# One row scatter under way at a time on POOL in a fused two-layer kernel with routed experts

## The chip, the cores and the metric

The kernel runs on 1 core of one Trainium2 chip. The metric is the device time in microseconds (us) of one execution; the number quoted for a kernel is the median of its runs.

## The reference

Two transformer-like layers over `x` of shape (4, 1024, 128) in f32, each with an adaptive layernorm ahead of its two halves. In both layers the second half is a mixture of experts with top-2 routing over 8 experts:

```
# layer 0: causal attention with 16 heads, then
scores = softmax(x @ gate_w.T); w = scores * top2_mask(scores)
out = sum_e w[:, e] * down_e(silu(gate_e(x)) * up_e(x)) + sigmoid(x @ sgate) * shared(x)
# layer 1: a state-space block (S4D kernel, FFT convolution, GLU), then
scores = x @ Wg.T; w = scores of the top 2
out = sum_e w[:, e] * W3_e(silu(W1_e x) * (W2_e x))
```

There are 4096 tokens, so 8192 rows (token, choice) go to experts in each layer. The change concerns only how these rows reach the experts.

## The kernel before, in words

The kernel computes only the two experts that a token chose. It does so by sorting rows in memory. Each of the 4 batches (1024 tokens, `TPB` = 8 tiles of 128 tokens) is normalised into `w.h[0]` (rows of 130 words: 128 values, an id and a weight), copied to `w.h[1]` by ACT (`second_copy`, which counts `h_kept`), scored on PE, and DVE works out for each row its place in the row store `d.xg[layer]` (`places`, which counts `slots_done`). Then POOL issues `scatter(pool, n)` for n = 0 to 63: one indirect DMA each, that takes 128 rows of 520 bytes from SBUF and writes each to its place in DRAM. Sixteen of them belong to a batch and count on one semaphore `scattered[b]`, 16 for each. The first of a batch waits for `h_kept` and `slots_done`; the other fifteen wait for nothing.

The experts (`experts_parts`) then run over `NSLOT` = 72 slots of 128 rows, in order. SP loads slot n into `xt` (line 1725), eight slots ahead at most (it waits for `y_done`, n - 7). It may start on the slots of a wave only when all batches of that wave are scattered: `WAVES` is [(2, 40), (3, 72)] for layer 0 (slots 0 to 39 need batches 0 to 2) and [(1, 24), (2, 40), (3, 72)] for layer 1 (slots 0 to 23 need batches 0 and 1). PE transposes the slot (`t_in`, L1844), makes gate and up products (L1852 in layer 0, L1858 in layer 1), ACT the silu, DVE the product (`product(n)`, L1795 and following, which first copies the ids of the rows to `place[:, n % 8]`), PE the down product (L1869), ACT scales into `yo[n % 8]` (`y_copy(n)`, L1767), and POOL scatters `yo` to `d.yk` (`experts.scatter`, L1738). `place` and `yo` have 8 buffers, so `product(n)` and `y_copy(n)` wait until y scatter n - 8 has landed:

```
after(dve, y_out[n % UN], 16 * (n // UN))   # product(n)
after(act, y_out[n % UN], 16 * (n // UN))   # y_copy(n)
```

PE, DVE and ACT take the steps of all slots in a fixed order, with one or two slots between the stages; in layer 0 the first 12 slots also carry the rest of the shared expert (`late_tensor` and its like), work that stands in the same fixed order.

The order on POOL sets what is queued behind a scatter. In layer 0 all 64 row scatters come first and the 72 y scatters after them. In layer 1 `ROWS_AHEAD` = 40 row scatters come first, then y scatter n and row scatter 40 + n take turns:

```
ahead = 2 * NT if layer == 0 else ROWS_AHEAD
for n in range(ahead):
    routed.scatter(pool, n)
for n in range(NSLOT):
    experts.scatter(pool, n)
    if ahead + n < 2 * NT:
        routed.scatter(pool, ahead + n)
```

Of the kernel before, what the change touches and what calls it, by code (L numbers as in the profile page):

```python
# [18 lines left out]
TPB = T // P  # L19
# [1088 lines left out]
def route_parts(nc, w, d, layer, ctx, bank, gate):  # L1108
# [57 lines left out]
    scattered = w.scattered[layer]  # L1166
# [71 lines left out]
    def scatter(pool, n):  # L1238

        t, k = divmod(n, 2)  # L1240
        b = t // TPB
        if n % (2 * TPB) == 0:
            pool.wait_ge(h_kept, b + 1)
            pool.wait_ge(slots_done, b + 1)
        nc.gpsimd.indirect_dma_start(out=d.xg[layer], out_offset=bass.IndirectOffsetOnAxis(ap=w.slot[:, k, t:t + 1], axis=0),  # L1245
                                     in_=w.h[k][:, t, :], in_offset=None).then_inc(scattered[b], 16)

# [411 lines left out]
    made.hid_done = hid_done  # L1659
    made.sync, made.gpsimd, made.vector, made.scalar, made.tensor = sync_part, gpsimd_part, vector_part, scalar_part, tensor_part  # L1660
    made.scatter, made.tables, made.tail, made.tails_out = scatter, tables, tail, tails_out
    made.tables_set, made.ranked, made.w_read, made.w_copied, made.sh_out = tables_set, ranked, w_read, w_copied, sh_out
    return made
# [1153 lines left out]
```

## Time and profile before

| what | us |
|---|---|
| median of 3 runs (1256.02 to 1265.23) | 1263.59 |
| the profiled execution, its own time | 1261.72 |
| its span, first to last instruction | 1260.2 |
| PE busy | 962.0 (76%) |
| DVE busy | 830.9 (66%) |
| ACT busy | 695.9 (55%) |
| POOL busy | 444.4 (35%) |

The rows are times of one profiled execution in us from the start of its span. 1.5 us of its time lie outside the span. An engine's share is an average over attention (to about 540 us), layer 0's routing and experts (to about 833), the state-space block (to about 935), layer 1's routing (to about 1047), its experts (to about 1233) and the last sums.

### The profile page before, as it was taken

The page shows a single profiled execution, that of the slowest core. Times are in us where ns is not written, and L with a number is a line of the kernel's source. Part 1 is how long each engine was busy: PE and PEld are TensorE (multiplying, and loading weights), DVE is VectorE, ACT ScalarE, POOL GpSimd, SP SyncE. Part 2 cuts the span into 40 slices and gives each one's busy share as a digit, 9 for nine tenths or more (in the row PEclk, how much of TensorE's full clock was granted, in tenths as well). Part 3 has the DMA queues.
Part 4 walks back from the last instruction along what each step waited for, and adds up shares of the span by engine and source line. Part 5 has one row for each costly group of instructions (what it writes and reads, how often), then busy time and mean ns, then how long its engine had stood idle before and what let it go on. Part 6 is the DMA issues. An engine that isn't in the chain of part 4 may idle for free. (4 is left out here: it accounts for less than half of the span.)

```text
span 1260.2 us, 26930 instructions
## 1 busy us (share of the span) xinstructions
PE 962.0 (76%) x9019; PEld 631.0 (50%) x9019; DVE 830.9 (66%) x2082; ACT 695.9 (55%) x1479; POOL 444.4 (35%) x510
## 2 busy tenths in 40 slices
PE   4565899999999999957748977827578446779990
PEld 2232343333434333445436766727455336779990
DVE  6797998999999999376523445447867444323445
ACT  3684477877877777734324555528024333446660
POOL 5617122323212221216652356520001462664441
PEclk9795699999999999966779989868778657999995
DMA  7236011111111100021111122257552321222226
GB/s 208 67 110 226 7 61 53 51 35 49 53 38 36 46 8 2 2 72 61 45 53 33 43 78 77 69 195 228 137 149 64 87 71 31 63 76 69 66 57 208
DMA packets 101694, 97.16 MB, mean 77 GB/s; under 512 B 15181, under 2 KB 85928, under 8 KB 101560
## 3 DMA queue, kind: packets, MB, share of 16 engines
q1 hardware_dynamic: 87320, 75.29, 20.2%
q0 software_dynamic: 8704, 17.97, 4.2%
q10 hardware_dynamic: 5536, 2.18, 0.6%
q8 instruction: 76, 1.25, 0.4%
q14 instruction: 58, 0.48, 0.1%
HBM read 60.18 MB, written 34.95 MB: 75 GB/s over the span
## 5 line engine op out<-in xcount | busy, mean ns | idle before, releaser
L569 DVE TENSOR_REDUCE part<-sps 128x2 f32<-128x1024 f32 (+2 forms) x307 | 327.5, 1114 | 27.1 <-PE sps L557 15.3
L912 ACT ACTIVATE prob<-tpa 128x1024 f32<-128x1024 f32 (+1 forms) x208 | 192.8, 927 | 45.2 <-PE tpa L858 43.3
L1738 POOL DMA_INDIRECT yk<-yo,place x144 | 146.7, 1019 | 179.4 <-ACT yo L1767 162.0
L744 POOL TENSOR_SCALAR_AFFINE_SELECT prob<-prob 128x512 f32<-128x512 f32 x128 | 80.5, 641 | 307.2 <-ACT prob L912 307.2
L1245 POOL DMA_INDIRECT xg<-h,slot x128 | 127.7, 998 | 130.6 <-DVE slot L1396 88.9
L878 PE MATMUL ops<-prob,vs 128*32 128x512 f32 (+3 forms) x1536 | 157.9, 498 | 0.1
L912 ACT ACTIVATE prob<-tpb 128x512 f32<-128x512 f32 (+1 forms) x224 | 126.8, 566 | 36.5 <-PE tpb L858 36.4
L1795 DVE COPY place<-xt 128x1 uint32<-128x1 uint32 x144 | 22.1, 153 | 187.9 <-ACT esg L1761 97.4
L550 PE MATMUL sps<-qk 48*128 48x512 bf16 (+2 forms) x734 | 132.4, 338 | 12.6 <-DVE part L569 7.8
L1858 PE MATMUL banks<-xT,y 128*128 128x128 f32 x864 | 112.9, 282 | 21.2 <-ACT y L1752 13.9
L1858 PEld LDWEIGHTS banks<-xT,y 128*128 128x128 f32 x864 | 105.7, 197 | 24.9 <-ACT xT L1747 17.8
L858 PE MATMUL tpa<-qk 50*128 50x512 bf16 (+3 forms) x512 | 85.4, 324 | 5.2 <-ACT prob L912 5.1
L858 PE MATMUL tpb<-qk 50*128 50x512 bf16 (+3 forms) x256 | 82.5, 342 | 4.8 <-DMA qk<-mrow 3.5
L550 PEld LDWEIGHTS sps<-qk 48*128 48x128 bf16 x734 | 41.1, 94 | 73.4 <-DVE part L569 49.6
L1767 ACT ACTIVATE yo<-banks,xt 128x128 f32<-128x128 f32 x144 | 53.0, 368 | 42.8 <-PE banks L1869 34.1
L1852 PE MATMUL banks<-xT,up_at 128*128 128x128 f32 (+1 forms) x432 | 67.2, 296 | 5.1 <-DVE up_at L1789 3.0
L557 PE MATMUL sps<-half 64*128 64x128 bf16 x976 | 66.5, 207 | 0.0
L858 PEld LDWEIGHTS tpa<-qk 50*128 50x128 bf16 x512 | 28.0, 94 | 69.4 <-ACT prob L912 61.2
L1844 PE MATMUL banks<-ident,xt 128*128 128x128 f32 x144 | 41.8, 292 | 27.3 <-ACT xT L1747 12.6
L1852 PEld LDWEIGHTS banks<-xT,up_at 128*128 128x128 f32 (+1 forms) x432 | 58.4, 204 | 7.4 <-ACT xT L1747 4.5
L557 PEld LDWEIGHTS sps<-half 64*128 64x128 bf16 x976 | 51.6, 97 | 20.8 <-issue 2.0
L1761 ACT ACTIVATE esg<-banks 128x384 f32<-128x384 f32 x72 | 35.5, 493 | 47.4 <-PE banks L1858 41.5
(356 smaller groups left out, 1878.7 us busy)
## 6 DMA issues: line engine op xcount, KB each, us to landing
xt<-xg SPq DMA_DIRECT2D x144, 65.0 KB
qk<-term SPq DMA_DIRECT2D x24, 256.0 KB, 2.7
qk<-qk SPq DMA_DIRECT2D x64, 96.0 KB
arena<-kpad SPq DMA_DIRECT2D x6, 1024.0 KB, 11.0
powers<-powr SPq DMA_DIRECT2D x8, 516.0 KB, 5.3
powr<-powers SPq DMA_DIRECT2D x4, 1032.0 KB, 9.0
qk<-qk SPq DMA_DIRECT2D x64, 64.0 KB
h<-yk SPq DMA_DIRECT2D x8, 512.0 KB, 7.3
```

Of the source, the lines that this page charges most:

```text
L550: ins = nc.tensor.matmul(out[:, s, at * wd:(at + 1) * wd], qk[lo:lo + KR, 0, x, i * P:(i + 1) * P], qk[lo:lo + KR, 1, x, c0:c0 + wd], star ...
L557: ins = nc.tensor.matmul(out[:, s, (at + 1) * wd - P + 64 * u:(at + 1) * wd], w.half[lo:lo + 64, 0, u, :], w.half[lo:lo + 64, 1, u, 64 * u ...
L569: return nc.vector.tensor_reduce(to, src, AX.X, ALU.max, negate=True)
L744: nc.gpsimd.affine_select(out=blk, in_=blk, pattern=[[0, HQ], [1, P]], compare_op=ALU.is_ge, fill=0.0, base=0, channel_multiplier=-1).then ...
L858: ins = nc.tensor.matmul(slot_of(t, m)[:, bank, col:col + n], qk[t % 4][lo:lo + KR + 2, 1, x, j * P:(j + 1) * P], qk[t % 4][lo:lo + KR + 2 ...
L878: ins = nc.tensor.matmul(ops[32 * h:32 * h + 32, o0:o0 + n], vs[t % 2][:, j, h, :], prob[:, PBUF[c] * HQ + u, col:col + n], start=c in OPE ...
L912: nc.scalar.activation(prob[:, at:at + len(units), 0:n], slot_of(t, m)[:, :, 0:n], ACT.Exp, scale=float(HD) ** -0.5).then_inc(exp_done, 1)
L1245: nc.gpsimd.indirect_dma_start(out=d.xg[layer], out_offset=bass.IndirectOffsetOnAxis(ap=w.slot[:, k, t:t + 1], axis=0), in_=w.h[k][:, t, : ...
L1738: nc.gpsimd.indirect_dma_start(out=d.yk, out_offset=bass.IndirectOffsetOnAxis(ap=place[:, u:u + 1], axis=0), in_=yo[u][:], in_offset=None) ...
L1767: nc.scalar.activation(yo[n % UN][:], pd[n % 2], ACT.Copy, scale=xt[n % UN][:, C + 1:C + 2]).then_inc(y_done, 1)
L1852: ins = nc.tensor.matmul(pg[n % 2][0:cw, m * P:(m + 1) * P], up_at[n % WST][:, m * P:m * P + cw], xT[n % 4][:], start=True, stop=True)
L1858: ins = nc.tensor.matmul(out[:, m * P:(m + 1) * P], up_at[n % WST][:, (k * M + m) * P:(k * M + m + 1) * P], xT[n % 4][:], start=True, stop ...
```

## The change

Each row scatter but the very first of a layer waits, before it is issued, until the row scatter ahead of it has landed, that is until `scattered` of its batch has got the 16 counts of each scatter up to it. The y scatters get no wait, and no other wait is changed.

```diff
@@ -1242,6 +1242,8 @@
         if n % (2 * TPB) == 0:
             pool.wait_ge(h_kept, b + 1)
             pool.wait_ge(slots_done, b + 1)
+        if n > 0:
+            pool.wait_ge(scattered[(n - 1) // (2 * TPB)], 16 * ((n - 1) % (2 * TPB) + 1))
         nc.gpsimd.indirect_dma_start(out=d.xg[layer], out_offset=bass.IndirectOffsetOnAxis(ap=w.slot[:, k, t:t + 1], axis=0),
                                      in_=w.h[k][:, t, :], in_offset=None).then_inc(scattered[b], 16)
```

## Rows read from the trace of the kernel before

**Rows 1.** The page's groups of instructions, the two kinds of scatter on POOL.

```profile
L1738 POOL DMA_INDIRECT yk<-yo,place x144 | 146.7, 1019 | 179.4 <-ACT yo L1767 162.0
L1245 POOL DMA_INDIRECT xg<-h,slot x128 | 127.7, 998 | 130.6 <-DVE slot L1396 88.9
```

**Rows 2.** Timeline of POOL, layer 0: start, duration, what, [idle before <- releaser].

```profile
564.81 1.20 POOL L1245 DMA_INDIRECT xg<-h,slot  x1 [18.92 <-DVE slot L1396]
...
567.79 1.46 POOL L1245 DMA_INDIRECT xg<-h,slot  x1 [0.30 <-issue]
569.55 0.96 POOL L1245 DMA_INDIRECT xg<-h,slot  x1 [0.30 <-issue]
...
635.10 0.96 POOL L1245 DMA_INDIRECT xg<-h,slot  x1 [0.30 <-issue]
...
665.69 0.96 POOL L1245 DMA_INDIRECT xg<-h,slot  x1 [0.30 <-issue]
```

**Rows 3.** The chain that ended last, 1225 to 1240: start, duration, piece.

```profile
1232.57 2.23 DMA yk<-yo,place
...
1234.88 3.93 DMA h<-yk
```

**Rows 4.** Timeline of all engines around two wakings of POOL.

```profile
645.76 0.17 DVE L1396 CAST slot<-slf 128x16 uint32<-128x16 f32 x1
...
646.72 0.96 POOL L1245 DMA_INDIRECT xg<-h,slot  x1 [10.66 <-DVE slot L1396]
...
672.82 0.37 ACT L1767 ACTIVATE yo<-banks,xt 128x128 f32<-128x128 f32 x1 [0.34 <-PE banks L1869]
...
673.46 0.96 POOL L1738 DMA_INDIRECT yk<-yo,place  x1 [6.81 <-ACT yo L1767]
```

**Rows 5.** Timeline of SP: first loads of slots, layer 0 and layer 1.

```profile
638.83 8.54 SPq L1725 DMA_DIRECT2D xt<-xg  x8
...
1026.74 2.60 SPq L1725 DMA_DIRECT2D xt<-xg  x3
```

**Rows 6.** Timelines of PE, ACT and DVE, layer 0's first slots.

```profile
655.57 0.27 PE L1844 MATMUL banks<-ident,xt 128*128 128x128 f32 x1
664.52 1.62 PE L1852 MATMUL banks<-xT,up_at 128*128 128x128 f32 x6
...
675.54 0.27 ACT L1747 COPY xT<-banks 128x128 f32<-128x128 f32 x1 [0.40 <-PE banks L1844]
...
696.38 0.15 DVE L1795 COPY place<-xt 128x1 uint32<-128x1 uint32 x1 [1.11 <-ACT esg L1759]
```

**Rows 7.** Timeline of POOL, layer 1's row scatters and its first y scatter.

```profile
971.15 0.99 POOL L1245 DMA_INDIRECT xg<-h,slot  x1 [35.81 <-DVE slot L1396]
...
1023.19 0.96 POOL L1245 DMA_INDIRECT xg<-h,slot  x1 [0.30 <-issue]
...
1057.49 0.96 POOL L1738 DMA_INDIRECT yk<-yo,place  x1 [16.47 <-ACT yo L1767]
1058.75 0.96 POOL L1245 DMA_INDIRECT xg<-h,slot  x1 [0.30 <-issue]
```

**Rows 8.** Timelines of PE and DVE, layer 1's first slots.

```profile
1050.13 2.90 PE L1858 MATMUL banks<-xT,y 128*128 128x128 f32 x12 [2.30 <-DVE y L1789]
...
1074.34 0.13 DVE L1795 COPY place<-xt 128x1 uint32<-128x1 uint32 x1
```

**Rows 9.** DMA issues by line: KB each, median us to landing.

```profile
flip<-in_flip SPq DMA_DIRECT2D x1, 64.0 KB, 1.9
```

**Rows 10.** Timelines of ACT, PE and DVE: long idle times during trains of row scatters.

```profile
636.01 0.60 ACT L1464 ACTIVATE sg<-banks 128x512 f32<-128x512 f32 x1 [13.06 <-remote]
...
993.31 1.09 PE L1570 MATMUL banks<-ident,h 128*128 128x128 f32 x4 [13.23 <-issue]
...
1022.50 0.22 DVE L1349 COPY lg<-banks 128x64 f32<-128x64 f32 x1 [10.09 <-DMA kpad<-gate]
```

**Rows 11.** Two stretches of layer 1: length, busy PE, PEld, DVE, ACT, POOL, PEclk.

```profile
1057.00:1137.00 80.00, 61.45 (x491) 58.19 (x490) 27.23 (x98) 32.91 (x100) 48.58 (x49) 0.96 0.24 69
1137.00:1229.00 92.00, 91.44 (x820) 91.23 (x819) 37.65 (x128) 61.12 (x174) 42.50 (x44) 1.00 0.22 62
```

## The prediction

> **What bounds the kernel now.** I read the costliest groups first, for how much of POOL the scatters are: 128 row scatters of 998 ns mean and 144 y scatters [rows 1]. By the mean alone POOL is idle two thirds of the time, so the question is not its load but who waits for the last scatter of a train. For that I read POOL's timeline. Inside a train the row scatters follow one another with 0.96 us of work and 0.30 us between, 1.26 us apart; a few of the first take up to 1.46 us [rows 2]. A batch of 16 is gone in about 20 us. The next batch's places are ready later than that in every case, so POOL waits for DVE at each batch head (88.9 us in all, [rows 1]). The scatters are now hidden behind the routing.
>
> Then come the two readers of a train's end. SP's first load of a slot in layer 0 is issued at 638.83 [rows 5], 3.73 us after the last scatter of batch 2 was issued at 635.10 [rows 2]. PE transposes that slot only at 655.57, and the first products with it start at 664.52 [rows 6]: the routing of batch 3 and the shared expert fill the time, so there are some 15 us of slack before the transpose and 24 before the products. In layer 1 SP starts at 1026.74 [rows 5], 3.55 us after batch 1's last scatter (1023.19, [rows 7]), and the products start at 1050.13 [rows 8]: slack of some 20 us. The second reader is the y scatter behind all row scatters on POOL's queue. Layer 0's first y scatter starts at 673.46 [rows 4], after the last row scatter of 665.69 [rows 2]; layer 1's at 1057.49 [rows 7]. And `product(8)` waits for that first y scatter to land, at 696.38 in layer 0 [rows 6] and 1074.34 in layer 1 [rows 8]: slack of some 20 and 15 us.
>
> **The pitch under the change.** One row scatter may start only when the one ahead has landed. No row shows the landing of a row scatter, so I bound it. The last y scatter, of the same form and nearly the same size, starts at 1232.57 and its DMA piece lasts 2.23 us; SP issues what waited for it at 1234.88 [rows 3]. The 3.73 and 3.55 us above contain the landing and SP's own steps ahead of a load (it has a register to read), so they are upper bounds. POOL's waking adds to it. A y scatter that waits for one semaphore starts 0.27 us after ACT's copy ends (672.82 + 0.37 to 673.46, [rows 4]). A row scatter at a batch head, with several waits ahead of it, starts 0.79 us after the places (645.76 + 0.17 to 646.72, [rows 4]). The new wait stands alone ahead of 15 of 16 scatters, so I take the y scatter's 0.27. The pitch p is then 2.23 + 0.27 = 2.50 us in place of 1.26. Low end: 2.3, the 2.23 with hardly any waking. High end: 2.8, from waking at 0.6 or landings made later by the weight loads and by DVE (the 1.46 us scatter is such a one). A batch takes 40 us, twice what it took. The heads of layer 0's batches lay 27 us apart (564.81 to 646.72 for three, [rows 2, 4]), so from batch 1 on POOL no longer waits for DVE there: the whole train is 64 scatters in a row from 564.81.
>
> The Trainium skill has a fit for this, in "DMA: Bandwidth & Descriptors", section "Anatomy of one DMA — SWDGE (gpsimd) path": about 2.0 us fixed, mostly the receipt of the write, plus the bytes over 436 GB/s. For 66,560 bytes that would be 2.15 us, an estimate by that page, and the trace's 2.23 agrees within 0.1. By it the pitch would be 2.42 and the sum below some 7 us smaller.
>
> **Layer 0.** Two routes lead to the slots. *By SP:* the last scatter of batch 2 is the 48th and starts at 564.81 + 47 x 2.50 = 682.3. SP's load follows 3.73 later (686.0), lands 1.9 later, the time of another 64 KB load [rows 9] (687.9), and PE's transpose, ACT's copy of 0.27 each [rows 6] and their start-ups take 0.7: the products start at 688.6, where they started at 664.52. That is 24 us late. *By POOL's queue:* the 64th scatter starts at 564.81 + 63 x 2.50 = 722.3. The first y scatter is behind it, with no wait of its own left by then: it starts 1.27 later and lands 2.23 after that, at 725.8. `product(8)` waits for it; at 24 us late it would come at 720.5. So it is held 5 us more, and 29.4 against before. While DVE is held, PE can still do the transpose, the gate and up products and one down product that stand ahead in its order, and catches up 1.5 us of that. I take +28 us. The y scatters piled up then go at 1.27 apart against a slot pitch of 3.83 at that point and stop nobody. Batch 3 has landed long before slot 40 is asked for. Nothing later in layer 0 depends on row scatters, and no slack was on the way to layer 1, so all 28 us are carried on. As a function of the pitch this is the larger of 63p - 129.6 and 47p - 93.4: 15 at 2.3, 47 at 2.8.
>
> **Layer 1.** Times here are still those of before, without the shift. Batch 1's last scatter is the 32nd: 971.15 + 31 x 2.50 = 1048.7. SP's load 3.55 later (1052.2), landing 1.9 (1054.1), transpose, copies and the start of the products 1.3, since ACT also lays the up weights: 1055.4 against 1050.13 [rows 8], +5 us (31p - 72.2 in general: 0 at 2.3, where the slack is just used up, +15 at 2.8). The first y scatter comes after 40 row scatters at 971.15 + 39 x 2.50 + 1.27 = 1069.9, 12 us later than before, and lands at 1072.2; `product(8)` comes at 1074.34 + 5 = 1079.6 and does not wait. The remaining 24 row scatters take turns with y scatters: 1.26 us apart the pair takes 2.53 us (1057.49, 1058.75, [rows 7]), and the landing of the row scatter ahead is 2.23 + 0.27 = 2.50 after its start. The new wait is over as POOL gets to it. It is no cost at p = 2.50 and 24 x 0.3 = 7 us on POOL alone at 2.8, where the slots' pitch of 3.1 us leaves that much free. The pitch of 3.1 is 80 us over 491 matmuls / 19 a slot [rows 11]. Waves 1 and 2 need row scatters that are issued behind y scatters 7 and 23, ten slots before SP asks. No cost.
>
> **The sum.** 28 + 5 = 33 us on the profiled execution's 1261.72, 1295; against the median of 1263.59, which is 1.9 above it, 1297. I say 1296. With p = 2.3 it is 15 + 0, 1278; with p = 2.8 it is 47 + 15 = 62, 1324.
>
> **The rivals.** *A. POOL wakes slowly.* If the new wait costs what the batch head's does (0.79, [rows 4]) or the landing is seen only 3 us after the start, p is about 3.1. Then layer 0 loses 63 x 3.1 - 129.6 = 66 and layer 1 31 x 3.1 - 72.2 = 24: 1353. For it: row scatters have shown only this slow waking. Against: that one has more than one wait, and the y scatter with a single wait shows 0.27.
>
> *B. The long stalls go, and pay for it.* During the trains engines stand still for 10 to 13 us though the work that they wait for is done: ACT 13.06 until 636.01, PE 13.23 until 993.31, DVE 10.09 until 1022.50 [rows 10], and each ends near a train's end. If scatters in close succession hold up the other engines' signals or instructions, half the rate may free them. But the front of both layers is then bound by POOL's train, as above, so what is freed there is slack again. It could pay only among the slots: in layer 1 they take 3.1 us each while row scatters are mixed in, and 92 us over 820 matmuls / 19 = 2.13 us afterwards [rows 11]. If the whole difference on 24 slots is due to row scatters under way together with others, 24 x 1.0 = 24 us come back: 33 - 24 = 9, a time of about 1273. Against: the y scatters still overlap the row scatters there, and the rate is the same.
>
> *C. Faster than before.* A single scatter under way lands sooner than one in traffic, and the stalls of B go too. With POOL's train as the bound, the loss in layer 0 is gone at p = 2.0 (47 x 2.0 - 93.4 = 0.6), and layer 1 gains only as far as 31p - 72.2 is below zero. The sum is zero at p = 2.12, and at p = 1.9 it is -4 - 13 = -17, 1246. That needs a landing 1.6 us after the start, against 2.23 for a lone y scatter with nothing else on the queues [rows 3]. Hardly possible.
>
> *D. The wait is no wait.* If scatters land before POOL is done with them, nothing changes: 1264. The same row speaks against it.
>
> **How the numbers follow.** Forecast 0.79, A 0.10, B 0.05, C 0.02, D 0.04. A measurement of this kernel tells about 1% (12.6 us) from no change. Slower by over 1%: forecast and A, 0.89. Within 1%: B and D, 0.09. Faster: C, 0.02. The range is the forecast's bounds, 1278 to 1324, widened a little to 1274 below, toward B, and to 1328 above, toward A, which leaves out 0.2.
>
> **What the changed profile should show.** Row scatters 2.5 us apart, POOL's idle before each about 1.5 instead of 0.30, released by a DMA. Layer 0's train from 565 to about 723 without a gap for DVE, SP's first slot load near 686, the first gate and up products near 689, `product(8)` near 726 waiting for a DMA. Layer 0's last y scatter 28 us later than 831. In layer 1, relative to its first row scatter, the first products 5 us later. The stretch of mixed scatters unchanged at 3.1 us a slot. The attention stage unchanged. The prediction is wrong if the pitch is not near 2.5, if the slots after the trains run at another pitch than before, or if the 16 counts of a landing come later in traffic than for the lone scatter of the chain.

## The result and the profile after

The changed kernel takes 1327.48 us, median of 4 runs (1325.28 to 1328.07). The kernel before, run beside it, takes 1261.66. The ratio is 1.052, with a 95% interval of 1.049 to 1.056. The change makes the kernel 5% slower. The profiled execution has a span of 1325.6 us against 1260.2, 65.4 us more.

POOL first. The page's groups of the two scatters, of the changed kernel; the rows of before are [rows 1]. The line numbers are 2 higher than before, since the change adds two lines.

```profile
L1247 POOL DMA_INDIRECT xg<-h,slot x128 | 125.5, 981 | 245.5 <-DMA xg<-h,slot 181.4
L1740 POOL DMA_INDIRECT yk<-yo,place x144 | 146.3, 1016 | 133.3 <-ACT yo L1769 111.4
```

The scatters themselves cost what they did. What stood in front of a row scatter was DVE's slots, for 88.9 us; now it is the landing of the scatter ahead, for 181.4 us. The timeline of POOL in layer 0, to be held against [rows 2]:

```profile
562.93 1.20 POOL L1247 DMA_INDIRECT xg<-h,slot  x1 [18.93 <-DVE slot L1398]
...
568.31 0.96 POOL L1247 DMA_INDIRECT xg<-h,slot  x1 [1.57 <-DMA xg<-h,slot]
572.54 0.96 POOL L1247 DMA_INDIRECT xg<-h,slot  x1 [3.27 <-DMA xg<-h,slot]
...
732.77 0.96 POOL L1247 DMA_INDIRECT xg<-h,slot  x1 [1.75 <-DMA xg<-h,slot]
734.03 0.96 POOL L1740 DMA_INDIRECT yk<-yo,place  x1 [0.30 <-issue]
```

Half of the 63 steps in layer 0 are 2.57 us or shorter, but 12 are over 2.7: the scatter at 568.31 is followed only 4.23 us later. From the first to the 64th it is 169.84 us over 63 steps, a mean of 2.70. In layer 1 the first 32 take 88.36 us over 31 steps, 2.85. The chain that ended last runs through layer 1's train. It shows, for each scatter, the time from its start to its landing (the DMA pieces) and POOL's waking after it ("issue").

```profile
1010.09 2.31 DMA xg<-h,slot
1012.39 0.27 issue
...
1017.74 5.78 DMA xg<-h,slot
...
1028.86 4.57 DMA xg<-h,slot
...
1055.02 3.37 DMA xg<-h,slot
...
1072.30 2.29 DMA xg<-h,slot
...
1098.45 2.31 DMA xg<-h,slot
...
1101.78 1.82 DMA xt<-xg
```

A landing in quiet, with nothing else on the DMA queues, is 2.27 to 2.31 us after the start; POOL's waking is 0.27. Three landings of layer 1 took 5.78, 4.57 and 3.37. The DMA queues of two stretches, with packets, MB and share of the 16 DMA engines, show what stands beside the first. From 1017 to 1024 SP has issued weight loads of 176 KB each (the first three rows; the loads are on q1); from 1072.3 to 1084 there is nothing but five scatters (the last row).

```profile
q1 hardware_dynamic: 1701, 1.04, 66.6%
q0 software_dynamic: 37, 0.07, 3.7%
q8 instruction: 1, 0.02, 0.9%
...
q0 software_dynamic: 128, 0.27, 7.2%
```

The readers of the train, layer 0, timelines of SP, PE and DVE (the last row is `product(8)`); before they stood at 638.83, 655.57, 664.52 and 696.38 [rows 5, 6].

```profile
691.88 0.37 SPq L1727 DMA_DIRECT2D xt<-xg  x1
...
693.83 0.45 PE L1846 MATMUL banks<-ident,xt 128*128 128x128 f32 x1 [65.01 <-DMA xt<-xg]
...
695.25 1.13 PE L1854 MATMUL banks<-xT,up_at 128*128 128x128 f32 x4
...
736.39 0.15 DVE L1797 COPY place<-xt 128x1 uint32<-128x1 uint32 x1 [11.84 <-DMA yk<-yo,place]
```

PE stands idle for 65 us for the first slot's rows. Then the engines work on eight slots, until DVE's `product(8)` waits 11.84 us for the first y scatter to land, which was queued behind all 64 row scatters.

Layer 1, timelines of PE, ACT and DVE around the first slots, and its two stretches of slots (columns as in [rows 11]). Before, the products began at 1050.13 [rows 8].

```profile
1105.87 1.41 PE L1860 MATMUL banks<-xT,y 128*128 128x128 f32 x5 [0.37 <-ACT y L1754]
...
1130.37 0.49 ACT L1763 ACTIVATE esg<-banks 128x384 f32<-128x384 f32 x1 [4.43 <-remote]
...
1143.30 0.49 ACT L1763 ACTIVATE esg<-banks 128x384 f32<-128x384 f32 x1 [8.60 <-remote]
...
1143.83 0.15 DVE L1797 COPY place<-xt 128x1 uint32<-128x1 uint32 x1 [10.51 <-ACT esg L1763]
...
1122.00:1202.00 80.00, 55.28 (x406) 51.86 (x405) 21.94 (x77) 28.33 (x85) 49.72 (x51) 0.86 0.23 67
1202.00:1295.00 93.00, 93.00 (x826) 93.00 (x826) 37.85 (x130) 60.71 (x172) 41.24 (x43) 0.99 0.21 60
```

In 80 us in which row and y scatters take turns PE now does 406 matmuls; before it did 491 [rows 11]. The stretch behind is the same: 93 us for 826. So the 65 us split by layer as follows. From layer 0's first row scatter to its last y scatter it was 266.43 us before and is 306.90 now, +40.5. In layer 1 it was 261.42 (971.15 [rows 7] to 1232.57 [rows 3]) and is 288.03 (1010.09 to 1298.12), +26.6. Layer 0's train itself began 1.9 us sooner.

One thing did get better. The times at which DVE has a batch's slots ready, in layer 1, in the changed kernel:

```profile
1009.07 0.17 DVE L1398 CAST slot<-slf 128x16 uint32<-128x16 f32 x1
...
1056.43 0.17 DVE L1398 CAST slot<-slf 128x16 uint32<-128x16 f32 x1
```

The first and the fourth are shown; they are 47.4 us apart, where the profile of before has 76.5 (970.13 to 1046.67). Another profile of the kernel before, taken with the experiments, gives 74.4 for the same:

```profile
963.26 0.18 DVE L1396 CAST slot<-slf 128x16 uint32<-128x16 f32 x1
...
1037.66 0.17 DVE L1396 CAST slot<-slf 128x16 uint32<-128x16 f32 x1
```

The routing of layer 1 is 27 to 29 us shorter (in layer 0 57.6 us in place of 82.1), and the slots do not start sooner for it, since SP's first load waits for POOL's train.

### The profile page after: what moved, and what is told of

It is laid out like the page before. It is cut to its first block and busy times, and to the rows that moved or that the text cites. A ratio compares the mean times of both kernels' runs of the same rounds, so it can differ in the third digit from the quotient of the medians.

```text
span 1325.6 us, 26930 instructions
## 1 busy us (share of the span) xinstructions
PE 957.3 (72%) x9019; PEld 624.8 (47%) x9019; DVE 829.0 (63%) x2082; ACT 696.5 (53%) x1479; POOL 440.3 (33%) x510
## 3 DMA queue, kind: packets, MB, share of 16 engines
q10 hardware_dynamic: 5536, 2.18, 0.6%
## 5 line engine op out<-in xcount | busy, mean ns | idle before, releaser
L1247 POOL DMA_INDIRECT xg<-h,slot x128 | 125.5, 981 | 245.5 <-DMA xg<-h,slot 181.4
L1860 PE MATMUL banks<-xT,y 128*128 128x128 f32 x864 | 115.7, 286 | 21.5 <-ACT y L1754 13.1
L1860 PEld LDWEIGHTS banks<-xT,y 128*128 128x128 f32 x864 | 108.4, 201 | 24.9 <-ACT xT L1749 22.6
L1749 ACT COPY xT<-banks 128x128 f32<-128x128 f32 x144 | 37.6, 261 | 120.1 <-PE banks L1846 117.3
L858 PE MATMUL tpa<-qk 50*128 50x512 bf16 (+3 forms) x512 | 85.5, 324 | 5.2 <-ACT prob L912 5.1
L1846 PEld LDWEIGHTS banks<-ident,xt 128*128 128x128 f32 x144 | 21.1, 147 | 137.7 <-issue 132.7
L550 PEld LDWEIGHTS sps<-qk 48*128 48x128 bf16 x734 | 41.2, 94 | 73.7 <-DVE part L569 50.1
L1871 PE MATMUL banks<-down,y 128*128 (+1 forms) x432 | 62.7, 281 | 3.4 <-issue 3.4
```

Of the source, the lines that this page charges most:

```text
L550: ins = nc.tensor.matmul(out[:, s, at * wd:(at + 1) * wd], qk[lo:lo + KR, 0, x, i * P:(i + 1) * P], qk[lo:lo + KR, 1, x, c0:c0 + wd], star ...
L858: ins = nc.tensor.matmul(slot_of(t, m)[:, bank, col:col + n], qk[t % 4][lo:lo + KR + 2, 1, x, j * P:(j + 1) * P], qk[t % 4][lo:lo + KR + 2 ...
L1846: nc.tensor.transpose(pT[n % 2], xt[n % UN][:, 0:C], w.ident[:]).then_inc(in_ps, 1)
L1860: ins = nc.tensor.matmul(out[:, m * P:(m + 1) * P], up_at[n % WST][:, (k * M + m) * P:(k * M + m + 1) * P], xT[n % 4][:], start=True, stop ...
L1871: ins = nc.tensor.matmul(pd[n % 2], hid[n % WST][0:cw, m, :], wt[0:cw, m, :], start=m == 0, stop=m == M - 1)
```

## The experiments

The runs came in four groups, each on a chip of its own. The kernel before took 1256.93 us (19 runs) in the first, 1154.54 (7) in the second, 1256.92 (13) in the third and 1156.62 (11) in the fourth. So there are two kinds of chip here, called the first kind (1257) and the second or quick kind (1155); the pair of the result, at 1262, is of the first kind. Each ratio below is against the kernel before on the same chip; spans and single times are compared within a kind of chip only, except where the text compares the kinds. All edits are to the changed kernel, unless it says otherwise.

### The wait in one layer only (first group)

```diff
-        if n > 0:
+        if n > 0 and layer == 0:      # the second run: layer == 1
```

> Only layer 0's row scatters wait for the landing ahead. My theory (the cost of each layer is its own train's length, less the slack ahead of the slots) expects 1261.7 + 40 = about 1301: the changed kernel's layer 1 began its row scatters 38.9 us later than before. In the profile product(8) of layer 0 waits for the first y scatter's landing near 736, and layer 1 looks as before. A rival, that the two layers' costs are not independent (traffic or clock carried over), would give something clearly away from 1301.

> Only layer 1's row scatters wait. My theory expects 1261.7 + 26 = about 1288: 17 us of it before the first products (the train of 32 at a mean pitch of 2.85 us against the routing), 10 us among the first slots, where POOL works off the y scatters that piled up. Together with the layer-0-only kernel the two costs should add up to the whole 66 us, within 4.

Layer 0 alone: 1298.1 (1293.61 to 1302.12), ratio 1.031 (1.026 to 1.037), 41.2 us. Layer 1 alone: 1282.11 (1281.12 to 1285.49), ratio 1.021 (1.015 to 1.026), 25.2 us. Together they are 66.4, which is the whole change within the spread of the runs. The layers' costs add up, and they agree with the +40.5 and +26.6 read from the trace. With layer 0's front as it was, layer 1 alone shows a like loss among its slots: from the first products to the last y scatter it takes 190.1 us (1061.80 to 1251.91), where the kernel before needs 182.4.

### Two row scatters under way, and a wait ahead of every second one (first group)

The first keeps two under way. A row scatter waits for the landing of the last but one; as the two halves k of a tile alternate, each half counts on a semaphore of its own.

```diff
-        if n > 0:
-            pool.wait_ge(scattered[(n - 1) // (2 * TPB)], 16 * ((n - 1) % (2 * TPB) + 1))
+        if n > 1:
+            pool.wait_ge(scattered[(n - 2) // (2 * TPB)][k], 16 * ((n - 2) % (2 * TPB) // 2 + 1))
```

> Each row scatter waits for the landing of the one before the last, so two may be under way (each batch's counts split over two semaphores, by the choice k). Theory: the cost is the landing latency in series; with two under way the pitch is the larger of 1.27 and 2.54 / 2 = 1.27, so no change: 1262 within 6 us, with the long idle times of the routing stages as before. Rival (the long idle times of the other engines come from an unbounded number of scatters under way): the routing stage of layer 1 shortens from 76 us to under 60, and the time falls by 10 us or more.

It took 1251.54 (1245.02 to 1261.41), ratio 0.996 (0.992 to 0.999), within the 6 us of this group's kernel before. POOL's timeline in layer 0:

```profile
575.68 0.95 POOL L1247 DMA_INDIRECT xg<-h,slot  x1 [0.58 <-DMA xg<-h,slot]
576.94 0.95 POOL L1247 DMA_INDIRECT xg<-h,slot  x1 [0.30 <-issue]
578.22 0.95 POOL L1247 DMA_INDIRECT xg<-h,slot  x1 [0.33 <-DMA xg<-h,slot]
```

A landing of 2.3 us and a waking of 0.27 make 2.57 us, just over two pitches of 1.26. So with two under way nearly every wait is over as POOL comes to it. So a wait and its semaphores cost nothing here; what costs is that only one scatter is under way. The routing is not freed either: in layer 1 the slots of the four batches still take 74.2 us (964.67 to 1038.88).

The second leaves out every other wait:

```diff
-        if n > 0:
+        if n > 0 and n % 2 == 0:
```

> Only every second row scatter waits for the landing ahead, so they come in pairs, 3.81 us a pair, a mean pitch of 1.9 us. Theory (the train's length against the routing that frees up at a lower rate of scatters): the last needed scatter of layer 0 comes at 564.8 + 23 x 3.81 + 1.27 = 653.7 and the first products at about 660 against 664.5; in layer 1 the first products come 14 us earlier than before: together 5 + 14 = 19 us faster, about 1243 (1235 to 1255). Rival (the routing stages speed up only if scatters are strictly one at a time): they stay at about 82 and 76 us and the time is that of before, 1262, within 6 us.

It took 1257.14 (1250.25 to 1262.34), ratio 1.000 (0.997 to 1.003), where 1243 was expected. The time is the rival's, but the rival's reason, a routing that stays as it was, is not what happened. The routing is freed as expected: layer 1's four batches of slots take 49.5 us (966.50 to 1016.02). But the train came out slower than the pairs at its start suggest:

```profile
967.52 0.99 POOL L1247 DMA_INDIRECT xg<-h,slot  x1 [34.37 <-DVE slot L1398]
968.81 0.97 POOL L1247 DMA_INDIRECT xg<-h,slot  x1 [0.30 <-issue]
971.40 0.96 POOL L1247 DMA_INDIRECT xg<-h,slot  x1 [1.61 <-DMA xg<-h,slot]
```

A pair is 3.88 us, so 1.94 a scatter; the first 32 took 67.6 us (967.52 to 1035.16), 2.18 each. The products begin 75.06 us after the first scatter, 3.9 sooner than before and not 14. Of the 27 us of routing that this frees, POOL's train gives 4 on; in layer 0 the products begin only 0.5 us sooner (99.24 after the first scatter against 99.71), and not 5. My expectation had taken the landings in quiet for all of them; most of its error in time is that.

### Every third, more row scatters behind the y scatters, fewer weight loads, an earlier wave (second group)

This chip runs the kernel before in 1154.54 us. No profile of the kernel before was taken on it.

```diff
-        if n > 0:
+        if n > 0 and n % 3 == 0:
```

> The new wait stands ahead of every third row scatter only, so three may be under way and the next group starts when the last of them has landed. Theory (spacing frees the routing, but the train then sets the end): the mean pitch is (2 x 1.26 + 2.5)/3 = 1.68 us, or some 1.9 with the late landings that the run with every second wait showed; no train is then later than the fronts need. If the long stalls of the routing go with the pauses, its fourth batch has its slots 25 us after the first scatter minus nothing: the last slots_done at about 622 in layer 0 and 1018 in layer 1 as with every second wait, and the first products of layer 1 come near 1038, the time 1245 to 1250. Rival (the stalls depend on how many row scatters are under way at once): with three under way the last slots come at about 645 and 1046 as in the kernel before, and the time is that of before, 1257.

1189.86 (1186.44 to 1192.71), ratio 1.031 (1.027 to 1.035). Both theories had 1245 or more, on a chip like the first. Against this chip's own time, the kernel is 3% slower though it waits ahead of only one scatter in three. Neither theory's time holds here. The slots of layer 1's four batches take 51.9 us (932.34 to 984.25), but that does not decide for the theory: on a quick chip the routing takes 49.2 us even with two scatters always allowed under way (fourth group, below).

```diff
-                ahead = 2 * NT if layer == 0 else ROWS_AHEAD
+                ahead = 48 if layer == 0 else ROWS_AHEAD
```

> The changed kernel, but in layer 0 48 of the 64 row scatters stand ahead of the first y scatter on POOL's queue in place of all 64; the other 16 take turns with the y scatters. Theory (layer 0's loss is the larger of two routes, and the one by POOL's queue is 11 us longer than that by SP's first load): product(8) is held no more until the first y scatter lands at 736, layer 0's first products stay at about 695, its last y comes 7 to 10 us sooner, and the time is about 1319 in place of 1327. Rival (turns of y and row scatters cost among the slots what layer 1 showed, some 0.4 us a slot or more): the 16 turns give the gain back, and the time stays within 3 us of 1327.

1276.54 (1275.14 to 1280.98), ratio 1.107 (1.102 to 1.111). The changed kernel without this edit wasn't run on this chip. Its nearest relative is the next one, which has the same queue in layer 0. There the first y scatter starts at 733.05 and `product(8)` at 735.41; here they stand at 701.42 and 724.65. DVE's timeline shows it, first in this kernel, then in the next:

```profile
724.65 0.15 DVE L1797 COPY place<-xt 128x1 uint32<-128x1 uint32 x1 [1.11 <-ACT esg L1761]
```

```profile
735.41 0.15 DVE L1797 COPY place<-xt 128x1 uint32<-128x1 uint32 x1 [12.03 <-DMA yk<-yo,place]
```

The wait of 12 us is gone, and `product(8)` comes when the slots' own pitch brings it. From the first row scatter to the last y scatter of layer 0 it is 273.3 us (563.20 to 836.51) against 288.9 (561.16 to 850.08). The products begin 131.0 and 132.0 us after the first row scatter, so 1.0 of the 15.6 is not the queue's. The route by POOL's queue costs some 14 us over SP's on this chip, and the 16 turns between the slots did not eat that up. The 14 is rough, since the two kernels differ in their weight loads too. Those are also why the whole times differ by only 5.3 us: with half the loads layer 1 is 8.6 us shorter (261.9 against 270.5). In the first pair of profiles it is less: the first products are 32.6 late and the end of layer 0 40.5, so 7.9, where 16p - 36.2, the difference of the prediction's two lines, gives 7.0 at 2.70. Both routes exist, and the one by POOL's queue is the longer.

```diff
             if e >= WB:
-                sp.wait_ge(w_tr, place(e - WB) + 1)
+                return
```

The last run of this kind leaves out the weight loads of experts 4 to 7 (and counts `w_in` without them).

> The changed kernel without the weight loads of experts 4 to 7 in both layers; their slots use the weights of experts 0 to 3, so the output is another one. All scatters, waits and products stay. Theory (the landings that take 3.4 to 5.8 us instead of 2.3 are late because of weight loads that SP issues during a train): the pitch falls to 2.55 throughout, the 32nd scatter of layer 1 starts 79 us after its first instead of 88, the 64th of layer 0 161 us after its first instead of 170, and the time is about 1327 - 9 - 9 = 1309. Rival (they are late because of instruction fetches or of something else): the late landings stay, the mean pitch stays at 2.70 and 2.85, and the time at 1322 to 1328.

1281.87 (1279.36 to 1284.47), ratio 1.110 (1.106 to 1.114). In layer 1 the first 32 row scatters take 83.25 us (990.03 to 1073.28), 2.69 each; with all the loads, in the kernel just above, 87.33 (975.50 to 1062.83), 2.82 each. POOL's longest idle time inside layer 1's train fell from 3.96 to 3.03, first with all the loads, then with half:

```profile
988.45 0.96 POOL L1247 DMA_INDIRECT xg<-h,slot  x1 [3.96 <-DMA xg<-h,slot]
```

```profile
1009.94 0.96 POOL L1247 DMA_INDIRECT xg<-h,slot  x1 [3.03 <-DMA xg<-h,slot]
```

These are single profiles, and the same 32 scatters take 88.36, 85.51 and 86.23 in the other three profiles with all the loads and every wait in layer 1. So weight loads are 2 to 5 us of the lateness in layer 1, where I had put 9. In layer 0 the first 48 take 125.0 us without these loads and 124.2 with them: there they are none of it. At 568.31 and 1055.02 in the changed kernel's profile the late landing comes with fetches of instructions on the DMA queues, two and one, and no load at all. There the two coincide; no run took the fetches away, so that they are the cause is not shown.

```diff
-WAVES = [[(2, 40), (NB - 1, NSLOT)], [(1, 24), (2, 40), (NB - 1, NSLOT)]]
+WAVES = [[(1, 24), (2, 40), (NB - 1, NSLOT)], [(1, 24), (2, 40), (NB - 1, NSLOT)]]
-        if n > 0:
+        if n > 0 and n % 2 == 0:
-                ahead = 2 * NT if layer == 0 else ROWS_AHEAD
+                ahead = ROWS_AHEAD
```

> The wait stands ahead of every second row scatter, layer 0 takes layer 1's waves (slots 0 to 23 need only batches 0 and 1) and has 40 row scatters ahead of its first y scatter as layer 1 has. Theory (with spaced scatters the routing of layer 0 is over 25 us sooner, and what was still waited for is the wave's table and batch 2's landing): the first products of layer 0 start near 640 in place of 664, and with 24 row scatters mixed in at up to 1 us a slot at most half of that is given back: time 1232 to 1245. Rival (the shared expert and the weights' preparation on PE and ACT set the start of the slots, or the mixed turns cost all of it): 1252 to 1260.

1193.35 (1192.92 to 1197.22), ratio 1.034 (1.030 to 1.039). The first products of layer 0 started at 635.47, even sooner than the 640 expected. But the times expected were those of the first chip, and against this chip's kernel before the result is a loss.

### The kernel before with a profile, the changed one again, the earlier wave alone (third group)

These were to tell whether the chips differ in how they bear scatters. The chip of this group turned out to be of the first kind.

> The kernel before, unedited, with a profile, beside the changed kernel in the same group: two groups of runs found the kernel before at 1257 and at 1155 us on two chips, and only the first has its profile. Theory (on the second chip row scatters 1.26 us apart don't hold up the other engines): if this group's time of before is near 1155, its profile shows the slots of layer 1's four batches in some 50 us as in the changed kernel, not in 76, no idle times of 10 to 13 us in the routing, and DVE's product(8) with slots at about 2.1 to 2.4 us each right away. Rival (the second chip is quicker in the transfers or in the products themselves): the routing takes 76 us there too and the time is gained evenly over the slots. If this group's time is near 1257, the profile is that of before within 5 us at each step.

> The changed kernel, unedited, on this group's chip. Theory (the train's pitch of 2.7 to 2.85 is the same on every chip, since it is one scatter's landing; what is held up in the kernel before is not): where the kernel before takes 1257, 1.052 times that, 1323; where it takes 1155, about 1155 + 125 = 1280, ratio 1.10 to 1.12. Rival (the cost is a fixed 66 us): 1.057 times 1155, 1221.

The kernel before: 1253.91, span 1252.4, with the first products and the last y scatter of both layers within 3.1 us of the first profile's, counted from the layer's first row scatter (74.4 us of routing, above). The changed kernel: 1322.55 (1321.59 to 1326.41), ratio 1.051 (1.047 to 1.056). So the cost repeats on another chip. Its products-to-last-y stretch in layer 1 is 190.1 us against 183.6 in this profile of before, +6.5; in the first pair it was +9.8. What the quick chips' profile of the kernel before would show stays open.

The earlier wave, put into the kernel before, without a wait:

```diff
-WAVES = [[(2, 40), (NB - 1, NSLOT)], [(1, 24), (2, 40), (NB - 1, NSLOT)]]
+WAVES = [[(1, 24), (2, 40), (NB - 1, NSLOT)], [(1, 24), (2, 40), (NB - 1, NSLOT)]]
-                ahead = 2 * NT if layer == 0 else ROWS_AHEAD
+                ahead = ROWS_AHEAD
```

> The kernel before with layer 1's waves and its 40 row scatters ahead of the first y scatter in layer 0 too, and no new wait. Theory (the start of layer 0's slots waits for the wave's table and for batch 2; an earlier wave opens them sooner): the first products of layer 0 start 10 to 20 us sooner than in the kernel before; where the scatters hold up the engines (a chip at 1257) the mixed turns give half of it back and the time is 1245 to 1255; on a chip at 1155 it is 1140 to 1150. Rival (PE's order keeps batch 3's routing ahead of the first slot, so the table was never waited for): no change beyond 5 us.

1254.58 (1251.87 to 1263.34), ratio 0.999 (0.996 to 1.002). The first products of layer 0 start 85.5 us after the first row scatter (564.53 to 650.07), where the profile of before in this group has 97.2 (561.79 to 658.96). The last y scatter comes at 260.9 against 263.4. So 12 us are gained at the start and 9 given back, by the windows of both: first this kernel, then the kernel before, over the same 935 matmuls.

```profile
650.00:825.00 175.00, 139.69 (x935) 119.93 (x934) 78.42 (x327) 88.94 (x315) 99.46 (x95) 0.93 0.23 64
```

```profile
659.00:825.00 166.00, 138.37 (x935) 117.83 (x934) 78.30 (x327) 88.86 (x315) 78.77 (x75) 0.94 0.22 60
```

With 20 more scatters among the slots they take 9 us longer, which is 0.45 us each if the whole difference is theirs.

### Two under way with the earlier wave (fourth group)

> Two row scatters may be under way at a time, and layer 0 takes layer 1's waves and its 40 row scatters ahead of the first y scatter. Theory (both edits alone moved the time by less than half a per cent where the kernel before takes 1257, the first mostly in layer 1, the second 7 to 10 us at the start of layer 0's slots, given back by the turns behind it): 1247 to 1253 there. On a chip where the kernel before takes 1155, with two under way the train is as fast as before, so nothing is lost: 1145 to 1155. Rival (even two under way cost POOL what the late landings add, as every third wait cost 3.1% on the chip at 1155): 1257 or more there, 1180 on the quick chip.

1169.88 (1167.38 to 1174.18), ratio 1.012 (1.009 to 1.014), on a chip of the second kind. The expected 1145 to 1155 is missed; there is a small loss, about half of what the rival's 1180 asks, and no run tells what makes it. With it there is one kernel's layer 1 on both kinds of chip, for the code of layer 1 is that of the first run with two under way. DVE's slots in layer 1 here:

```profile
922.96 0.18 DVE L1398 CAST slot<-slf 128x16 uint32<-128x16 f32 x1
...
972.17 0.17 DVE L1398 CAST slot<-slf 128x16 uint32<-128x16 f32 x1
```

and there:

```profile
964.67 0.17 DVE L1398 CAST slot<-slf 128x16 uint32<-128x16 f32 x1
...
1038.88 0.18 DVE L1398 CAST slot<-slf 128x16 uint32<-128x16 f32 x1
```

49.2 us against 74.2. And the slots of layer 1, row and y scatters in turns and then y scatters alone, first here:

```profile
1011.00:1069.00 58.00, 57.69 (x517) 57.48 (x516) 24.62 (x82) 37.78 (x108) 42.74 (x46) 1.00 0.36 94
1070.00:1140.00 70.00, 69.58 (x621) 69.20 (x620) 28.52 (x97) 45.69 (x130) 31.73 (x34) 1.00 0.21 60
```

then there:

```profile
1050.00:1128.00 78.00, 57.54 (x472) 54.25 (x470) 26.03 (x95) 32.32 (x99) 47.58 (x49) 0.98 0.24 70
1130.00:1222.00 92.00, 92.00 (x818) 92.00 (x817) 37.66 (x128) 60.14 (x170) 40.61 (x44) 0.99 0.21 61
```

The last stretches agree, 11.3 and 11.2 us for 100 matmuls. In the mixed stretch the quick chip has PE as full as there (57.69 of 58 us, 11.2 for 100), while the other needs 16.5 for 100. So the quick chip isn't quicker at this work. It does not show the standstills: neither in the routing with two scatters under way, nor among the slots.

This also accounts for the second group. Where nothing stands still, spacing the scatters has nothing to give back. From a layer's first row scatter to its last y scatter this kernel takes 220.0 and 217.2 us in the two layers. The kernel with 48 ahead, which waits for every landing, takes 273.3 and 270.5 on the other quick chip, 53 more in each. With the 13 by which this kernel is over the kernel before, that is 120 of the 122 us that it loses. Among the slots of layer 1 the loss is another one than on the first kind. There the wait holds POOL, and POOL holds the products. In the mixed stretch from 1087 to 1157 DVE's `product` waits 18 times, 38.8 us in all, for a y scatter to land, where this kernel's (991 to 1051) waits once, for 1.2. One of the 18:

```profile
1097.88 0.15 DVE L1797 COPY place<-xt 128x1 uint32<-128x1 uint32 x1 [2.00 <-DMA yk<-yo,place]
```

No version beat both kernels on both kinds of chip. The best against the kernel before is two under way, 0.4% faster where it was measured and not distinguishable from a change of nothing by the 1% of this kernel's measurement.

## Why the prediction was right, and where its terms were off

**The pitch.** Landing plus waking is what the chain shows: 2.31 and 0.27 at the head, 2.29 and 0.27 in quiet. Predicted were 2.23 and 0.27. Two things came on top. A landing of a row scatter in quiet is some 0.06 us longer than that of the last y scatter, so the pitch in quiet is 2.53 to 2.57. And some landings are late, up to 5.78 us. The means, 2.70 in layer 0 and 2.85 in layer 1, are the mis-sized term; the high end had been set at 2.8 for this reason. The Trainium skill's fit, in "DMA: Bandwidth & Descriptors", section "Anatomy of one DMA — SWDGE (gpsimd) path", gave 2.15 us, an estimate by that page. The landing in quiet is 0.14 over it, and for a landing while 176 KB loads fill two thirds of the DMA engines the trace has more than twice that.

**Layer 0.** The forecast was +28 at a pitch of 2.50, by 63p - 129.6. At the measured 2.70 the formula gives 40.5; measured are 40.5 in the trace and 41.2 in the run with the wait in layer 0 only. SP's route, 47p - 93.4, gives 33.5 at 2.70; the first products came 32.6 later (99.71 to 132.32 after the first scatter). Both routes come out as predicted, and the longer one by POOL's queue was named. The run with 48 scatters ahead shows it: the hold of `product(8)` goes, and the end of layer 0 comes sooner. The small allowance of 1.5 us for PE's catching up wasn't tested alone.

**Layer 1.** The forecast was +5 at 2.50, by 31p - 72.2. At 2.85 it is 16.2, and the products came 16.8 later. That is the same mis-sized pitch. The other part is a missed step: "no cost" for the turns of row and y scatters. The slots took 9.8 us more, 7.7 more in the run with layer 1 alone (190.1 against 182.4), and 6.5 more in the third group. The prediction asked only whether POOL would have time for its waits, and there it was right: POOL's pairs go at 2.5 to 3.0 us (one from 1122.84 to 1125.82), within the slots' 3.1. It didn't ask what the backlog does. The first y scatter comes 17.0 us after the first products (1105.87 to 1122.84) and not 7.4 (1050.13 to 1057.49, [rows 7, 8]), so more y scatters are waiting by then. POOL works them off without a pause, 14 scatters in a row some 1.3 us apart (1122.84 to 1139.85), and in that time PE, ACT and DVE have long idle times, DVE's of 10.51 us among them:

```profile
1134.85 2.90 PE L1860 MATMUL banks<-xT,y 128*128 128x128 f32 x12 [6.41 <-ACT y L1754]
...
1139.85 0.95 POOL L1247 DMA_INDIRECT xg<-h,slot  x1 [0.32 <-issue]
1144.33 0.96 POOL L1740 DMA_INDIRECT yk<-yo,place  x1 [3.52 <-ACT yo L1769]
```

These twelve matmuls end at 1137.75, yet ACT's silu of them starts only at 1143.30, after the last scatter of the run. Counted from the first products, `product(8)` is 0.8 us later than before and `product(9)` 8.0, so nearly the whole loss lies in this one place. It has the look of the standstills in the routing. PE's granted clock adds to it: it fell from 1.00 (2.4 GHz) to 0.50 (1.2 GHz) during PE's idle time of 6.41 us, and these twelve matmuls took 2.90 us where twelve at full clock took 1.57 (at 1126.08). The size of the loss goes with the lateness of the first y scatter. At 7.4 to 10.2 us after the first products (before, two under way, every second) the slots take 182.4 to 184.7 us, at 16.2 to 17.6 (the three profiles with every wait on this kind of chip) 190.1 to 192.3. No run changed the backlog alone, so that it is the cause is argued, not shown: the waits in the turns are a rival that these same runs do not separate from it.

**The sum.** 28 + 5 = 33 were forecast and 65 came: 12.5 of the difference are layer 0's pitch, 11 or 12 layer 1's, and 10 the slots of layer 1, less the 1.9 by which the first train began sooner. That 1327.48 still lies in the range, 0.5 us under its upper bound of 1328, is in part luck. By the prediction's two formulas the measured pitches give 40.5 + 16.2 = 57 us, some 1318. The other 9 us are for the most part the slots of layer 1, which the prediction had at nothing, and they fit only because its top of 1324 was taken at a pitch of 2.8 in both layers and then widened toward rival A.

**Rival B, the long stalls.** Its mechanism is true in part. The standstills in the routing do vanish when the scatters are spaced (47.4 us between the first and the last slots of layer 1, in place of 76.5), and two under way are already enough to keep them (74.2). As the prediction said, the train then sets the end and the relief is slack. It does not pay among the slots; there it went the other way. **Rival A** had a pitch of 3.1 from slow waking; the waking is 0.27 at nearly every step. **Rivals C and D** are out by the landing of 2.3 us: not under 2, and not nothing.

**What it could not have known** from one profile: the size of the loss depends on the chip. With the kernel before at 1155 us, the changed kernel with fewer loads or a shorter queue is at a ratio of 1.11. There the step "no cost" for the turns fails by the wait itself: with PE free of standstills the slots come faster than POOL's turns.

## What to carry to other kernels

A wait for a transfer's landing turns a queue's pitch from the issue time into landing plus waking, here from 1.26 into 2.53 us and more; multiply it by the length of the train and compare with each reader's slack, the readers further down the same queue too, for these were the costlier ones here. Take the landing from the busiest stretch in which the train runs, not from a lone transfer at the kernel's end: a few landings at twice the time and many slightly late ones were 0.2 us on the mean in layer 0 and 0.3 in layer 1, and over 63 and 31 steps that was some 20 us. If a queue is to be thinned out, allow two under way first; that cost nothing on one kind of chip and, with another edit in it, 1.2% on the other.

## What the runs showed of the hardware

Row scatters 1.26 us apart go with standstills of the other engines on the first kind of chip, two of the four of the experiments and that of the first pair: the routing of layer 1 takes 74 to 77 us in the kernel before and with two under way, and 47 to 52 us when every second scatter or each one waits for a landing. The two others didn't show it: one of them took 49.2 us with the same code of layer 1 in place of 74.2, and the other was not run with two under way or none held back. There the kernel before ran in 1155 us and not 1257, 8% less. What lies between the layers ran alike on both kinds (139.9 us from layer 0's last y scatter to layer 1's first row scatter in the kernel before, 140.0 in the kernel with half the loads), and so did layer 1's last stretch. Layer 0's slots with y scatters alone did not: 743 matmuls in 110 us in the kernel with half the loads, 700 in 120 us in the changed kernel on a chip of the first kind. The missing loads are not the reason: with all of them, the kernel that waits for every third takes 112.9 us from `product(8)` to layer 0's last y scatter, the one with half the loads 114.7, and the kernels on the first kind with y scatters alone there 131.8 to 134.9. That y scatters hold the others up too, in layer 0, fits this, but no run took them away or spaced them. What differs in these chips, and how a scatter comes to hold up another engine, the runs don't tell.
